# Three quarters of a weight load, issued behind the last residual stores instead of ahead of them, at the turn from one stage to the next

## The chip, the cores and the metric

The kernel runs on one core of a Trainium2 chip, as one launch. What counts is the device time of the execution, in microseconds (us). The core has five engines with a program each: TensorE (matmuls and transposes, called PE in the profile), VectorE (DVE), ScalarE (ACT), GpSimd (POOL) and SyncE (SP), which here only issues DMAs. ScalarE issues some DMAs too. All DMAs go through the core's 16 DMA engines. The engines wait for each other by semaphores.

## What is computed

The input x has 16 sequences of 1024 tokens, 512 features each, float32. A layer norm gives xn; the output is x plus a state-space block of xn plus a sparse expert block of xn:

```python
x = L0_attn_x
xn = _layernorm(x, axis=-1)
x = x + _L0_attn_ref(xn, W_in, dt_W, dt_b, A_log, D_param, W_out, norm_w) \
      + _L0_ffn_ref(xn, Wc, bc, W1, b1, W2, b2)
```

The second block takes the tokens in groups of 32. In each group each of 32 x 4 = 128 experts picks the token with its highest logit, by a one-hot matrix:

```python
logits = jnp.einsum('bntd,des->bntes', grouped, Wc) + bc
perm = (logits == jnp.max(logits, axis=-3, keepdims=True)).astype(x.dtype)
permuted = jnp.einsum('bntd,bntes->bnesd', grouped, perm)
inner = jax.nn.relu(jnp.einsum('bnesd,esdf->bnesf', permuted, W1) + b1)
result_permuted = jnp.einsum('bnesf,esdf->bnesd', inner, W2) + b2
result = jnp.einsum('bnesd,bntes->bntd', result_permuted, perm)
```

The first block ("attention" in the names of the code) is a projection, a scan over chunks of 64 tokens, a gate, a norm and an output projection.

## The kernel before

The kernel has three stages, one after the other in every engine's program: attention (to about 2070 us), gather (to about 2480 us) and scatter.

**Attention** walks over 64 super tiles of 256 tokens (NST = 64, two tiles of 128 each, 128 tiles in all), as a pipeline of three super tiles: at step s the projections of s, the scan of s - 1 and the output projection of s - 2. The last two steps, s = 64 and 65, only drain it. Per super tile it leaves in HBM: xn (normalised tokens, `xn_dram`), the one-hot matrix (`permT_dram`) and x plus the block's result, called the residual (`part_dram`). The residual of tile n is made by VectorE (`residual`, line 880) from output projection n into buffer `res[:, i]`, i = n mod 2, and SP stores it (`store_part`, line 368). The next residual into the same buffer waits until that store has landed (`res_out[i]`). Store (62,0) is that of tile 124, store (62,1) that of 125, (63,0) and (63,1) those of 126 and 127.

**Gather** works in 8 blocks (NGB) of 2048 tokens. A wave n = 4b + k is block b and the k-th of four slices of 128 features (KD = 4), so there are 32 waves. SP loads the tokens of a wave in four parts (tq) of four DMAs each, 64 KB apiece (`load_xn`, line 1292), into one of four buffers. TensorE's `pick` (n, tq) (line 1448, its matmuls at line 1462) multiplies a part by the one-hot matrix, 32 matmuls into one bank of PSUM; ScalarE (line 1389) and VectorE (`move_pick`, line 1391, copy at line 1393) each copy half of it to SBUF, and the next pick waits for both copies. Behind pick (n, tq) TensorE multiplies the picks of wave n - 1 by a slice of W1 (`apply_w1`, line 1469, matmuls at line 1486). W1, 8 MB, is loaded once, in four quarters by feature slice, 2 MB each (`load_w1`, line 1300). `apply_w1` of wave k waits for quarter k at its first use: quarter 0 behind pick (1,0), quarter 1 (the diff's k = 1) behind pick (2,0), and so on. The texts below count quarters 1 to 4 and waves 1 to 4 in words: quarter 2 of W1 is `load_w1(sync, 1)`, and the third wave is n = 2. In SBUF, W1 takes the place of attention's weights, so no quarter may be loaded before the last logits are projected (`lg_ps`).

**The turn.** The first picks are put between the last output projections: TensorE's order at the end is pick (0,0), transposes, projection 126, pick (0,1), projection 127, then pick (0,2), transposes of the second block's one-hot matrix (line 1445), pick (0,3), pick (1,0). VectorE's order is: copy of pick (0,0), residual 126, copy of pick (0,1), residual 127, copy of pick (0,2). The second block's transposes also wait for the last residual.

SP issues its DMAs in program order, and a wait in its program holds back all that is behind it. Its order at the turn, before the change: one-hot matrices of the first two blocks (8 DMAs), the first wave's tokens (16), quarter 1 of W1, the last store of the one-hot matrix, then `load_second`: the second wave's tokens (16) and quarters 2 to 4 of W1. Behind these come the four residual stores, each with its wait for the residual. The gather's own program (`sync_program`, line 1332) begins with waits for the last store of the one-hot matrix and for the last residual (`res_cp` at 2 * NST). Then come the tokens of the third and fourth waves, the permutation of the third block, and the loop that loads wave n + 4 as pick n goes on.

Of the kernel before, what the change touches and what calls it, by code (L numbers as in the profile page):

```python
# [31 lines left out]
KD = D // P  # L32
# [30 lines left out]
def wait(eng, sem, value):  # L63

    if not isinstance(value, int) or value > 0:
        eng.wait_ge(sem, value)
# [1154 lines left out]
def gather_phase(nc, io, keep, sems, att):  # L1221
# [67 lines left out]
    def quarter(i):  # L1289
        return slice(P // 4 * i, P // 4 * (i + 1))  # L1290

    def load_xn(sync, n, tq, i):
        tiles = slice(TW * tq, TW * tq + TW)
        sync.dma_start(xn[n % 4][quarter(i), tiles, :],
                       xn_dram[n // KD, n % KD][quarter(i), tiles, :]).then_inc(xn_in[n % 4][tq], 16)

    def load_perm(sync, b, i):
        sync.dma_start(permT[b % 2][quarter(i), :, :], perm_dram[b][quarter(i), :, :]).then_inc(perm_in[b % 2], 16)

    def load_w1(sync, k):  # L1300
        sync.dma_start(w1[:, k, :, :], io["w1"][:, k, :, :]).then_inc(w1_in[k], 16)
# [17 lines left out]
    def load_second(sync):  # L1319
        for tq in range(4):  # L1320
            for i in range(4):
                load_xn(sync, 1, tq, i)
        for k in range(1, KD):
            load_w1(sync, k)

    def store_inner(eng, b, piece):

        quads = slice(PQ * piece, PQ * piece + PQ)
        eng.wait_ge(biased, 2 * b + 1 + 2 * piece // PIECES)
        eng.dma_start(inner_dram[b][:, quads, :], inner[b % 2][:, quads, :]).then_inc(inner_out[b % 2], 16)  # L1330

    def sync_program(sync, scatter):
        for i in range(2):
            sync.wait_ge(att["pm_out"][i], 16 * (NST // 2))
        sync.wait_ge(att["res_cp"], 2 * NST)
        for n in range(2, 4):
            for tq in range(4):
                for i in range(4):
                    load_xn(sync, n, tq, i)
        sync.wait_ge(perm_ps, 1)  # L1340
        for i in range(4):
            load_perm(sync, 2, i)
        for e in range(4 * LAST):
            b, w = divmod(e, 4 * KD)
            sync.wait_ge(pick_ps, e + 1)
            for i in range(4):
                if i == 1:
                    wait(sync, w1_mid, e - 3)
                if i == 2:
                    sync.wait_ge(pick_cp[0], e + 1)  # L1350
                if i == 3 and e + 1 < 4 * LAST:
                    sync.wait_ge(pick_mid, e + 2)
                if e + 16 < 4 * LAST:
                    load_xn(sync, e // 4 + 4, e % 4, i)
            if b == NGB - 1 and w % 4 == 3:
                scatter["load_first"](sync, w // 4)
        for piece in range(PIECES // 2):
            store_inner(sync, NGB - 1, piece)
        for w in range(2):
            scatter["load_w2_next"](sync, w)  # L1360
        for piece in range(PIECES // 2, PIECES):
            store_inner(sync, NGB - 1, piece)
        for w in range(2, 4):
            scatter["load_w2_next"](sync, w)
# [103 lines left out]
    def tensor_program(pe, scatter):  # L1468
# [38 lines left out]
        for j in range(4):  # L1507
            scatter["apply_w2"](pe, j)
            apply_w1(LAST - 1, j)

    return dict(sync=sync_program, gpsimd=gpsimd_program, scalar=scalar_program, vector=vector_program, tensor=tensor_program,
                load_small=load_small, load_first=load_first, load_second=load_second, load_w1=load_w1, negate_b1=negate_b1,
                cast_ident=cast_ident, copy_perm=copy_perm, copy_pick=copy_pick, move_pick=move_pick, pick=pick,
                transpose_picks=transpose_picks,
# [370 lines left out]
```

## Time and profile before

| | |
|---|---|
| median of the runs | 3000.07 us |
| lowest and highest of the three | 2998.5, 3001.02 us |
| span of the profiled execution | 3002.6 us |
| TensorE busy (matmuls) | 2871.7 us, 96% |
| VectorE, ScalarE, GpSimd busy | 2053.3, 1713.5, 1430.4 us |
| DMA, mean over the span | 110 GB/s |

The profile is of one execution; all times are counted from the start of its span. Engines' busy times leave out register, semaphore and DMA-issuing instructions. TensorE's weight loads are an engine of their own in it (PEld). A row of a timeline gives the start, the duration, the engine, the line in the kernel, the operation with output and input, and how many instructions were merged; in brackets stands how long the engine was idle before and what ended that ("issue": nothing that the profile shows). SPq and ACTq are SP's and ScalarE's issues of DMAs; their duration is that of issuing, not of the transfer. Names with g_ belong to the gather and with s_ to the scatter; g_w is W1, g_xn a token buffer, g_picked the picks in SBUF.

### The profile page before, as it was taken

The numbers are of one execution on the slowest core, as the hardware profiler recorded it, in microseconds if no ns is written. First come the engines' busy times: TensorE is split into PE (matmuls) and PEld (weight loads), VectorE is DVE, ScalarE is ACT, GpSimd is POOL, SyncE is SP. The second block draws the span as 40 slices with busy tenths as digits, with TensorE's granted clock in tenths as the row PEclk, the third lists the DMA queues.
The fourth block names the chain that finished last, engine by engine and source line by source line (L and its number), as shares of the span: only waits on it lengthen the run. The fifth ranks groups of instructions, "written<-read, shape, count | busy, mean of one in ns | idle before, by whom it ended". The sixth has DMA issues, their size and how long they took to land.

```text
span 3002.6 us, 134681 instructions
## 1 busy us (share of the span) xinstructions
PE 2871.7 (96%) x59324; PEld 2453.1 (82%) x59324; DVE 2053.3 (68%) x2982; ACT 1713.5 (57%) x3751; POOL 1430.4 (48%) x2287
## 2 busy tenths in 40 slices
PE   8999999999999999999999999996787879999999
PEld 6888888888888888888888888885666668888887
DVE  5777777777777777777777777775444447777775
ACT  5665666666656666666566666663333335555555
POOL 4666676766666767667667666672010101101010
PEclk9999999999999999999999999998999999999999
DMA  4222222222222222222222222216444437877765
GB/s 150 77 74 71 77 78 75 76 74 77 74 71 79 76 76 76 70 80 74 72 79 74 80 71 71 81 46 214 131 134 119 115 110 217 235 218 223 225 206 156
DMA packets 372550, 328.99 MB, mean 110 GB/s; under 512 B 62960, under 2 KB 284656, under 8 KB 371328
## 3 DMA queue, kind: packets, MB, share of 16 engines
q1 hardware_dynamic: 362016, 310.21, 35.6%
q8 instruction: 469, 7.68, 1.1%
q10 hardware_dynamic: 9952, 10.17, 1.1%
q14 instruction: 113, 0.93, 0.1%
HBM read 206.96 MB, written 113.31 MB: 107 GB/s over the span
## 4 chain that ended last, share of the span: by engine, by line
PE 90%; DVE 4%; issue 3%; DMA 1%; SPq 1%; POOL 1%; ACT 0%; ACTq 0%; DVEq 0%; POOLq 0%
PE a_proj L992 40%; PE a_mix L992 11%; PE s_rt L1748 8%; PE g_pick_ps L1462 5%; PE a_scan L1106 5%; PE s_w_ps L1716 5%; PE s_rt L1761 4%; DVE g_picked L1393 3%; PE a_scan L1083 3%; PE a_scan L1070 2%; PE g_acc_ps L1486 2%; PE a_mix L1058 2%; PE a_misc L1050 1%; PE a_misc L1124 1%; DMA part_dram<-res 1%
## 5 line engine op out<-in xcount | busy, mean ns | idle before, releaser
L992 PE MATMUL a_proj<-wdh,xTh 128*128 128x512 f32 x1024 | 420.9, 411 | 5.0 <-issue 3.1
L1679 ACT COPY s_res<-s_rt 128x512 f32<-128x512 f32 x512 | 262.9, 601 | 245.8 <-PE s_rt L1748 245.8
L992 PE MATMUL a_proj<-wdh,xTl 128*128 128x512 f32 x1024 | 402.0, 393 | 0.0
L992 PE MATMUL a_proj<-wdl,xTh 128*128 128x512 f32 x1024 | 400.0, 391 | 1.5 <-issue 1.5
L824 DVE COPY_PREDICATED scan_in<-mask,a_scan 64x512 f32<-64x512 uint32 x512 | 382.3, 747 | 16.0
L1693 DVE TENSOR_TENSOR s_resT<-s_w_ps,s_b 128x1024 f32<-128x1024 f32 (+1 forms) x252 | 293.1, 1205 | 136.4 <-PE s_w_ps L1716 136.4
L465 POOL TENSOR_TENSOR dx<-xs,d_row 64x512 f32<-64x512 f32 x256 | 330.3, 1290 | 15.1
L640 ACT ACTIVATE scan_in<-CT,hsel 64x128 f32<-64x128 f32 x1024 | 326.0, 388 | 4.9
L473 POOL TENSOR_TENSOR yv<-yt,dx 128x512 f32<-128x512 f32 x128 | 188.6, 1473 | 292.8 <-DVE yt L864 292.8
L604 ACT ACTIVATE raw<-a_proj,rs 128x272 f32<-128x272 f32 x128 | 62.5, 488 | 427.6 <-PE a_proj L992 427.6
L1393 DVE COPY g_picked<-g_pick_ps 128x1024 f32<-128x1024 f32 x128 | 156.7, 1224 | 216.3 <-PE g_pick_ps L1462 216.3
L884 DVE SCALAR_TENSOR_TENSOR res<-a_mix,rms,x 128x512 f32<-128x512 f32 x127 | 95.4, 751 | 270.9 <-PE a_mix L992 258.6
L456 POOL TENSOR_TENSOR scan_in<-CT,hsel 64x512 f32<-64x512 f32 x256 | 269.0, 1051 | 10.0
L1389 ACT COPY g_picked<-g_pick_ps 128x1024 f32<-128x1024 f32 x128 | 129.6, 1012 | 248.4 <-PE g_pick_ps L1462 247.8
L1748 PE MATMUL s_rt<-s_ident,s_resT 128*128 128x128 f32 x2048 | 254.7, 278 | 0.9 <-DVE s_resT L1693 0.5
L616 ACT ACTIVATE xs<-a_proj,rs 64x512 f32<-64x512 f32 x256 | 174.8, 683 | 125.0 <-PE a_proj L992 123.4
L1748 PEld LDWEIGHTS s_rt<-s_ident,s_resT 128*128 128x128 f32 x2048 | 219.0, 140 | 31.6 <-issue 25.1
L992 PEld LDWEIGHTS a_proj<-wdh,xTh 128*128 128x128 f32 x1024 | 192.2, 188 | 47.5 <-issue 10.8
L992 PEld LDWEIGHTS a_proj<-wdh,xTl 128*128 128x128 f32 x1024 | 192.3, 188 | 45.4 <-issue 1.9
L992 PE MATMUL a_proj<-xTh,wth 128*128 128x256 f32 x768 | 222.1, 289 | 0.0
L992 PEld LDWEIGHTS a_proj<-wdl,xTh 128*128 128x128 f32 x1024 | 193.0, 188 | 35.2 <-issue 2.9
L992 PE MATMUL a_proj<-xTh,wtl 128*128 128x256 f32 x768 | 216.3, 282 | 0.0
(153 smaller groups left out, 7104.4 us busy)
## 6 DMA issues: line engine op xcount, KB each, us to landing
x<-in_x_dram SPq DMA_DIRECT2D x128, 256.0 KB, 2.7
xn_dram<-xn SPq DMA_DIRECT2D x128, 256.0 KB, 2.4
part_dram<-res SPq DMA_DIRECT2D x128, 256.0 KB, 2.5
g_xn<-xn_dram SPq DMA_DIRECT2D x512, 64.0 KB, 2.3
s_w<-in_w_dram SPq DMA_DIRECT2D x128, 256.0 KB, 4.1
s_part<-part_dram SPq DMA_DIRECT2D x128, 256.0 KB, 3.9
out_dram<-s_out SPq DMA_DIRECT2D x128, 256.0 KB, 3.0
xr<-in_xT_dram SPq DMA_DIRECT2D x126, 256.0 KB, 2.8
```

Of the source, the lines that this page charges most:

```text
L456: nc.gpsimd.tensor_tensor(c_places(1, w), src, sel, ALU.mult).then_inc(cs_cp[1], 1)
L465: nc.gpsimd.tensor_tensor(dx[rows_, :], xs[c][n % 4][rows_, :, :].rearrange("t h d -> t (h d)"), d_row[rows_, :], ALU.mult).then_inc(dx_cp, 1)
L473: nc.gpsimd.tensor_tensor(yv[:], yt[:], dx[:], ALU.add).then_inc(yv_cp, 1)
L616: last = nc.scalar.activation(xs[c][n % 4][rows_, :, :], proj[0][rows_, :].rearrange("p (h d) -> p h d", h=H), ACT.Copy, scale=inv(n, rows_))
L640: last = nc.scalar.activation(dst[:, :, j, :], CT[own, n % 4, :, 0:CH], ACT.Copy, scale=hsel4[own, j:j + 1])
L824: nc.vector.copy_predicated(dst, mask[rows_, :].unsqueeze(1).unsqueeze(1).to_broadcast([CH, 4, 2, CH]), src).then_inc(mt_cp, 1)
L992: last = nc.tensor.matmul(out, lhs[a], rhs[c], start=(k == 0 and n == 0), stop=(k == nk - 1 and n == 2))
L1106: last = nc.tensor.matmul(out, scan_in[c][:, h, i:i + 32], xs[c][n % 4][:, h, :], start=True, stop=True)
L1393: nc.vector.tensor_copy(picked_view(n, tq, 1), pick_view(1)).then_inc(pick_cp[1], 1)
L1679: nc.scalar.copy(res[:, n % 4, :, :], rt_bank[:, n % 3, :, :]).then_inc(res_cp, 1)
L1693: last = nc.vector.tensor_tensor(resT[m % 2][j][:, :, sets].rearrange("p n (q r) -> p n q r", r=4)[:, :, :, 0:r], w2_place(u)[:, 0:r, :, j ...
L1748: last = nc.tensor.transpose(rt_bank[:, n % 3, g, :], resT[m % 2][j][:, place, :], ident[:])
```

## The change

`load_second` no longer issues quarters 2 to 4 of W1. The gather's program on SP issues them behind its waits for the last residual, the first of them ahead of the third wave's tokens, the second between the third and the fourth wave's, the third behind these. The set of DMAs is the same. No other engine's program changes.

```diff
@@ -1320,8 +1320,6 @@
         for tq in range(4):
             for i in range(4):
                 load_xn(sync, 1, tq, i)
-        for k in range(1, KD):
-            load_w1(sync, k)
@@ -1333,10 +1331,12 @@
         for i in range(2):
             sync.wait_ge(att["pm_out"][i], 16 * (NST // 2))
         sync.wait_ge(att["res_cp"], 2 * NST)
-        for n in range(2, 4):
-            for tq in range(4):
-                for i in range(4):
-                    load_xn(sync, n, tq, i)
+        for k in range(1, KD):
+            load_w1(sync, k)
+            if k < KD - 1:
+                for tq in range(4):
+                    for i in range(4):
+                        load_xn(sync, k + 1, tq, i)
         sync.wait_ge(perm_ps, 1)
```

## Rows read from the trace of the kernel before

**Rows 1.** The page, busy tenths of TensorE in 40 equal slices of the span.
```profile
PE   8999999999999999999999999996787879999999
```

**Rows 2.** Chain that ended last, 2040 to 2080 us: start, us, what.
```profile
2057.89 19.27 DMA part_dram<-res
```

**Rows 3.** Timeline of SP's issues, 2020 to 2120 us.
```profile
2047.43 0.43 SPq L1301 DMA_DIRECT2D g_w<-in_w_dram  x1
...
2056.47 1.37 SPq L1301 DMA_DIRECT2D g_w<-in_w_dram  x3
2057.89 22.67 SPq L370 DMA_DIRECT2D part_dram<-res  x4
2080.67 18.01 SPq L1294 DMA_DIRECT2D g_xn<-xn_dram  x32
```

**Rows 4.** DMA issues 2050 to 2060 us: count, KB each, median us to landing.
```profile
g_w<-in_w_dram SPq DMA_DIRECT2D x3, 2048.0 KB, 14.7
```

**Rows 5.** Timeline of VectorE at the turn.
```profile
2077.63 0.75 DVE L884 SCALAR_TENSOR_TENSOR res<-a_mix,rms,x 128x512 f32<-128x512 f32 x1 [12.31 <-DMA part_dram<-res]
2078.30 1.21 DVE L1393 COPY g_picked<-g_pick_ps 128x1024 f32<-128x1024 f32 x1
```

**Rows 6.** Timeline of TensorE at the turn.
```profile
2039.86 1.05 PE L1445 MATMUL g_acc_ps<-g_ident,g_permT 128*128 128x128 bf16 x16 [0.97 <-DMA g_permT<-permT_dram]
...
2070.13 0.40 PE L992 MATMUL a_misc<-woh,yll 128*128 128x512 f32 x1
2079.66 2.09 PE L1462 MATMUL g_pick_ps<-g_perm,g_xn 32*128 32x128 f32 x32 [9.13 <-DVE g_picked L1393]
...
2087.03 1.17 PE L1462 MATMUL g_pick_ps<-g_perm,g_xn 32*128 32x128 f32 x32 [1.44 <-DVE g_picked L1393]
```

**Rows 7.** Stretch of 2 us: PE busy, granted clock, DMA share, GB/s.
```profile
2076.00:2078.00 2.00, 0.00 (x0) 0.50 0.10 31
```

**Rows 8.** DMA issues in 2047.77 to 2048.71 us: KB each, us to landing.
```profile
g_w<-in_w_dram SPq DMA_DIRECT2D x1, 2048.0 KB, 10.4
...
g_xn<-xn_dram SPq DMA_DIRECT2D x1, 64.0 KB, 6.9
```

**Rows 9.** Timeline of TensorE in the gather's first waves.
```profile
2094.80 0.75 PE L1486 MATMUL g_acc_ps<-g_picked,g_w 128*32 128x64 f32 x36 [0.39 <-issue]
...
2096.59 1.08 PE L1486 MATMUL g_acc_ps<-g_picked,g_w 128*32 128x64 f32 x59
2099.13 0.31 PE L1486 MATMUL g_acc_ps<-g_picked,g_w 128*32 128x64 f32 x5 [1.46 <-issue]
2099.37 1.18 PE L1462 MATMUL g_pick_ps<-g_perm,g_xn 32*128 32x128 f32 x32
```

**Rows 10.** DMA by queue, 2100 to 2200 us: packets, MB, share of 16 engines.
```profile
q8 instruction: 25, 0.41, 1.9%
```

**Rows 11.** Waits of TensorE, 2100 to 2200 us: us in total, times, longest.
```profile
PE g_acc_ps L1486 <- issue: 9.6, 11, 2.1
...
PE g_pick_ps L1462 <- issue: 2.6, 4, 1.3
```

**Rows 12.** DMA 2060 to 2070 us, packets of all queues.
```profile
DMA packets 293, 4.16 MB, mean 416 GB/s; under 512 B 34, under 2 KB 34, under 8 KB 40
```

**Rows 13.** Timeline of TensorE as the scatter's first loads go out.
```profile
2435.08 0.95 PE L1462 MATMUL g_pick_ps<-g_perm,g_xn 32*128 32x128 f32 x23 [1.06 <-issue]
...
2439.42 0.99 PE L1486 MATMUL g_acc_ps<-g_picked,g_w 128*32 128x64 f32 x55 [0.50 <-issue]
...
2444.47 0.87 PE L1486 MATMUL g_acc_ps<-g_picked,g_w 128*32 128x64 f32 x24 [2.27 <-issue]
```

**Rows 14.** Stretch of 4 us: PE busy, granted clock, DMA share, GB/s.
```profile
2440.00:2444.00 4.00, 2.20 (x101) 1.00 0.99 340
```

**Rows 15.** DMA by queue, 2440.5 to 2444.5 us.
```profile
q1 hardware_dynamic: 646, 1.19, 81.9%
```

**Rows 16.** The page, DMA issues: count, KB each, median us to landing.
```profile
g_xn<-xn_dram SPq DMA_DIRECT2D x512, 64.0 KB, 2.3
```

## The prediction

> **What bounds the kernel now.** First the page's slices of 75 us: TensorE is busy nine tenths or more in attention and scatter and seven or eight tenths in the gather between; the lowest (6) is the slice from 2027 to 2102 us, the turn from attention to gather [rows 1]. The chain that ended last goes into the transfer of a residual store there and stays in it for 19.27 us [rows 2]. SP's timeline tells what lies before that store: the issues of W1's quarters 2 to 4, at 2056.47, with the first of four residual stores at 2057.89 [rows 3]. The three quarters land in a median of 14.7 us [rows 4], the store only after them: it stands in line behind 6 MB. VectorE's residual of tile 126 needs that store's buffer and sits idle 12.31 us for it, until 2077.63; behind it on VectorE is the copy of the picks (line 1393), and TensorE's pick (0,2) sits idle 9.13 us for that copy [rows 5, 6]. [...]
>
> **What the change takes away.** Without three W1 issues ahead of it, store (62,0) is issued at about 2056.5 instead of 2057.9. Only the first W1 quarter (issued 2047.43, 10.4 us, thus landed at 2057.8) and the second wave's tokens lie before it. It must land by 2066.3, when projection 126 is done; with the 6.9 us of a token load behind a quarter [rows 8] it lands at 2063.4. The other store before the end, (62,1), is issued at about 2059.1 and needed at 2070.5. No wait is left there.
> The new chain, each step from a row:
> - projection 127 ends at 2070.5 as before (last matmul 2070.13, 0.40) [rows 6]. Pick (0,2) follows at once, since its bank's copy is made while projection 127 runs: 2070.4 to 2071.5. I take full clock, as TensorE comes from four busy microseconds and more, with no gap before it.
> - residual 127 (0.75 us) to 2071.35; transposes of the second block 1.05 us as those at 2039.86, to 2072.5. VectorE's copy of pick (0,2) 1.22 us [rows 5, 6] after the residual, 2071.65 to 2072.9. Pick (0,3) 2073.1 to 2074.3, its copy to 2075.6, pick (1,0) at 2075.8.
> Before, pick (1,0) starts at 2087.03 [rows 6]. **The gain up to there is 11.2 us**: 9.3 of waiting (2079.66 against 2070.4) and 1.9 for work and clock. From pick (1,0) on the order of TensorE's work is the same in both.
>
> **What the change adds: the data.** No wait is new, but W1's quarters 2 to 4 now stand behind SP's wait for all residuals (about 2071.4), and the tokens of waves 3 and 4 stand between them.
> - SP issues a token load in 0.56 us (32 in 18.01) and a quarter in 0.45 (1.37 for three) [rows 3]. So quarter 2 goes out at 2071.9, 16 loads of wave 3 until 2081.4, quarter 3 there, 16 loads of wave 4 until 2090.9, quarter 4 there, four of the permutation until 2093.1, and then the loop for the fifth wave and on.
> - A quarter with a wave of tokens behind it landed in 10.4 us [rows 8]; those issued in a row in 14.7, the median [rows 4]. Quarter 2 lands at 2082.3 to 2086.6 and is first read behind pick (2,0), which is four picks after 2075.8. Before, these four took 12.34 us (2087.03 to 2099.37) [rows 6, 9], so quarter 2 is needed at 2089.3 at the earliest: 3 to 7 us to spare. Quarter 3 lands at 2091.8 to 2096.1, needed behind pick (3,0) at 2101 or later; quarter 4 at 2101.3 to 2105.6, needed behind pick (4,0), 2112 or later. Tokens of wave 3, part one: issued by 2074.6, landed at 6.9 us, 2081.5, needed at 2088. The loop's first load (wave 5) is issued at 2093.1 and needed at about 2111. Covered, all of them; if one isn't, TensorE, and behind it both copies, stand still for the remainder.
> - ScalarE issues four permutation loads of its own from pick (1,0) on. They aren't waited for before the ninth wave.
>
> **What the change adds: company for the code.** This is the term that I price against the gain. TensorE gets its instructions by DMA as well: the queue named instruction carried 25 packets with 0.41 MB from 2100 to 2200 us, 16.4 KB each [rows 10]. In the gather stage TensorE halts in the middle of a group, for "issue": at 2094.80, and again at 2099.13, with 36 matmuls, a pick of 32 and 59 more between, 127 in all [rows 9]. 127 matmuls with their weight loads are 254 instructions, a block of code. From 2100 to 2200 us these halts sum to 9.6 + 2.6 = 12.2 us [rows 11], 0.49 for each of the 25 packets. So in the gather the next block arrives just about when it is needed, and whatever slows its transfer is paid in full. (In the scatter TensorE is nine tenths busy or more [rows 1], so there it does not matter.)
> Before, W1 passed while TensorE ran the last projections or stood still, few instructions a microsecond. In the changed kernel it passes beside the densest code. From 2071.9 to about 2101 the DMA engines have 6 MB, which at 4.16 MB in 10 us [rows 12] is 15 us out of 29, and between them 32 and more token loads in small packets: about full.
> The nearest rows for a gather stage with full DMA are those where the scatter's first loads go out: 2434 to 2444, at the end with a share of 0.99. Its three halts are 1.06, 0.50 and 2.27 us, 1.28 each [rows 13, 14]. How many blocks begin in the loaded stretch? Pick (1,0) at 2075.8 to 2101, a block each 4.2 us: six. Six at 1.28 are 7.7 us; six at the 0.49 of before are 2.9. **The loss with traffic like that one is 4.8 us**; the low end is 0, if it was only the mix of queues there that did the harm. For the high end: packets of W1 are large, 4.16 MB in 293 [rows 12], 14 KB, where those of 2440 were 1.8 KB (1.19 MB in 646) [rows 15]. Sixteen engines for 10 us over 293 packets are 0.54 us a packet. One such packet ahead of each block adds 6 x 0.54 = 3.2, so 8.0 us; two make 11.3, the high end. I take the middle of 4.8 and 8.0, **6.4 us**, as the load of 2440 is the nearest and one packet ahead of a block the plainest addition. A clock that falls after a long halt, as at 2079.66 (0.9 us on one pick), costs 1 us more and is only in the range.
> Sum: -11.2 + 6.4 = -4.8 us. The profiled execution spans 3002.6 us, 0.08% above the median of 3000.07; I take the difference from the median: **2995.3 us**.
>
> [...] The halts [rows 9, 11] are there without W1 already. [...]
> [...] No row shows a code block behind a W1 packet.
>
> **Rivals.**
> 1. The code comes in time all the same. For it: the waits count 15 halts for 25 blocks [rows 10, 11], so ten blocks came in time. Against: the three halts at full share [rows 13]. Loss 0 to 3 us, time 2988.9 to 2991.9. Chance 0.22.
> 2. Code behind W1 (the slower side). If a block waits as a token load does behind a quarter, 6.9 us [rows 8] instead of 2.3 [rows 16], it comes 4.6 us later. [...] Place: blocks from 2076 to 2101 us. The point from which it decides: the kernel loses when six blocks lose over 11.2 us together, 1.9 each, and is slower by over 0.2% from 2.9 each. At 3.5 each, 21 us: 3010. Against it: the token loads stand in W1's own queue, code in another. Chance 0.10; a middle course (loss of 9 to 17 us, 2998 to 3006) 0.09.
> 3. A quarter or a wave lands late, as DMA is full and SP issues in order: at 5 us over the 14.7 [rows 4], quarter 2 would land at 2091.6, 2 us late, and the others likewise: 2997 to 3002. Against: no other quarter is ahead of it. Chance 0.05.
> 4. The change doesn't take: store (62,0) is still late behind quarter 1 and the tokens, as these share the engines until 2060 or so; then residual 126 waits as before. It would have to land 10 us later than the token loads beside it. 3000. Chance 0.04.
> The forecast (loss of 3 to 9 us, 2991.9 to 2998) has the remaining 0.50.
>
> **How the numbers follow.** What a measurement of this kernel can tell from no change is about 0.2%, 6 us: faster means below 2994.1, slower above 3006.1. Faster: rival 1 (0.22) and four tenths of the forecast (0.20), 0.42. Slower: rival 2 and a rest of the middle, 0.12. Same: 0.46. The range leaves out rival 2 and the top of the middle course: 2988.5 to 3003.
>
> **What the trace after would show.** The first step is right if VectorE's residual 126 starts at about 2066.4 without a wait for the residual store, and pick (0,2) at 2070.4, at full clock. The second, if pick (1,0) starts at about 2075.8. The third, if SP's issues of W1 lie at about 2072, 2081 and 2091 and TensorE waits for neither W1 nor tokens. The fourth, the price, if the halts for "issue" in the first 25 us from pick (1,0) sum to 8 to 11 us where six blocks of before have 2.9; at under 5 it is rival 1, at over 20 rival 2. From pick (5,0) on both kernels should run in parallel, with a constant offset of 5 us. The prediction is wrong if that offset changes later, or if a wait at the turn stays that I put down to the store.

## The result and the profile after

The changed kernel takes 3007.53 us (median of 20 runs), the kernel before, on the same chips, 3001.91 (20 runs): a ratio of 1.0017, 95% interval 1.0010 to 1.0023. That is 5.1 us slower on 3000: small, inside the 0.2% that was called no change, but clear of 1 by the interval, and in the other direction than forecast. 3000.07 x 1.0017 is 3005.2, which is 2.2 us above the end of the range (3003) and 9.9 above the forecast of 2995.3. The profiled execution spans 3005.8 us, against 3002.6 before.

The stores no longer stand in line. SP's issues at the turn (start, us, line, what, count):

```profile
2058.60 15.20 SPq L370 DMA_DIRECT2D part_dram<-res  x4
2073.92 0.43 SPq L1301 DMA_DIRECT2D g_w<-in_w_dram  x1
...
2082.71 0.43 SPq L1301 DMA_DIRECT2D g_w<-in_w_dram  x1
...
2091.24 0.43 SPq L1301 DMA_DIRECT2D g_w<-in_w_dram  x1
...
2093.57 36.24 SPq L1294 DMA_DIRECT2D g_xn<-xn_dram  x63
```

VectorE in the changed kernel: residuals 126 and 127 (line 884), which now wait for projections alone, and the copies of picks (0,2), (1,0) and (4,0).

```profile
2068.57 0.75 DVE L884 SCALAR_TENSOR_TENSOR res<-a_mix,rms,x 128x512 f32<-128x512 f32 x1 [1.14 <-PE a_mix L992]
2072.67 0.75 DVE L884 SCALAR_TENSOR_TENSOR res<-a_misc,rms,x 128x512 f32<-128x512 f32 x1 [1.74 <-PE a_misc L992]
2073.87 1.22 DVE L1393 COPY g_picked<-g_pick_ps 128x1024 f32<-128x1024 f32 x1 [0.45 <-PE g_pick_ps L1462]
...
2079.07 1.23 DVE L1393 COPY g_picked<-g_pick_ps 128x1024 f32<-128x1024 f32 x1 [1.38 <-PE g_pick_ps L1462]
...
2130.74 1.23 DVE L1393 COPY g_picked<-g_pick_ps 128x1024 f32<-128x1024 f32 x1 [2.44 <-PE g_pick_ps L1462]
```

The wait of 12.31 us [rows 5] is gone. The turn came 2.1 us later in this execution, which has nothing to do with the change: in attention, near 1000 us, the execution is already 1.8 us behind. So I count from VectorE's first copy of a pick, (0,0): it starts at 2063.10 before and at 2065.21 after. From there, the copy of pick (1,0) starts after 25.16 us before (2088.26) and after 13.86 now (2079.07): 11.3 us gained. But from the copy of (1,0) to that of (4,0), which I call **the stretch**, it was 35.49 us (2088.26 to 2123.75) and is 51.67 now (2079.07 to 2130.74): 16.2 us lost. From TensorE's timeline in the stretch:

```profile
2080.44 1.16 PE L1462 MATMUL g_pick_ps<-g_perm,g_xn 32*128 32x128 f32 x28 [0.40 <-DVE g_picked L1393]
2083.85 0.49 PE L1462 MATMUL g_pick_ps<-g_perm,g_xn 32*128 32x128 f32 x4 [2.25 <-issue]
...
2087.76 1.07 PE L1486 MATMUL g_acc_ps<-g_picked,g_w 128*32 128x64 f32 x28
2090.62 0.75 PE L1486 MATMUL g_acc_ps<-g_picked,g_w 128*32 128x64 f32 x36 [1.79 <-issue]
...
2092.41 1.08 PE L1486 MATMUL g_acc_ps<-g_picked,g_w 128*32 128x64 f32 x59
2098.20 0.43 PE L1486 MATMUL g_acc_ps<-g_picked,g_w 128*32 128x64 f32 x5 [4.71 <-issue]
2098.57 2.09 PE L1462 MATMUL g_pick_ps<-g_perm,g_xn 32*128 32x128 f32 x32
...
2105.09 0.50 PE L1462 MATMUL g_pick_ps<-g_perm,g_xn 32*128 32x128 f32 x6 [1.38 <-issue]
...
2112.70 1.13 PE L1486 MATMUL g_acc_ps<-g_picked,g_w 128*32 128x64 f32 x39 [4.00 <-issue]
2113.76 2.09 PE L1462 MATMUL g_pick_ps<-g_perm,g_xn 32*128 32x128 f32 x32
```

These lines answer to [rows 9]. The halts are in the middle of a group, and in the code TensorE's waits stand only ahead of one, so a wait for data isn't their cause. The longest is 4.71 us where 1.46 was; the five sum to 14.13 us. After three of them (2.25, 4.71 and 4.00 us) the next pick takes 2.09 us instead of 1.17, at a granted clock of 0.50; after the first, 68 matmuls at full clock lie between. Three stretches of 2 us, with TensorE's busy time, granted clock, DMA share and GB/s among the columns:

```profile
2082.00:2084.00 2.00, 0.15 (x3) 0.15 (x3) 0.00 (x0) 0.00 (x0) 0.00 (x0) 1.00 1.06 259
...
2096.00:2098.00 2.00, 0.00 (x0) 0.00 (x0) 0.00 (x0) 0.00 (x0) 0.00 (x0) 0.50 0.91 283
...
2110.00:2112.00 2.00, 0.00 (x0) 0.00 (x0) 0.00 (x0) 0.00 (x0) 0.00 (x0) 1.00 1.09 286
```

All engines but the DMA engines stand still. DMA issues from 2080 to 2085 us in the changed kernel (KB each, us to landing) show how long a transfer then takes, in SP's queue and in ScalarE's:

```profile
g_w<-in_w_dram SPq DMA_DIRECT2D x1, 2048.0 KB, 11.1
g_xn<-xn_dram SPq DMA_DIRECT2D x9, 64.0 KB, 6.3
g_permT<-permT_dram ACTq DMA_DIRECT2D x1, 128.0 KB, 8.2
```

The last line is the one I should have asked for: a load in another queue than W1's takes 8.2 us, where the median of such loads was 2.9 before, in the list of all DMA issues of the kernel:

```profile
g_permT<-permT_dram ACTq DMA_DIRECT2D x20, 128.0 KB, 2.9
```

The copy of pick (5,0) starts 73.08 us after the first copy before and 78.24 now, 5.2 us later. That this equals the 5.1 us of the ratio is luck, for the offset of these two executions doesn't stay: at the copy of pick (7,3) it is 2.8 us (112.02 against 109.22), at (15,3) 0.3 and at the last, (31,3), 1.4 (403.66 against 402.22). The spans differ by 3.2 us, 2.1 of them from before the turn. Single executions wander by 2 us and more in the rest of the gather; that the kernel lost about 5 us rests on the 20 runs of each, not on the two traces.

### The profile page after: what moved, and what is told of

It is laid out like the page before. It is cut to its first block, busy times and chain, and to the rows that moved or that the text cites. A ratio compares the mean times of both kernels' runs of the same rounds, so it can differ in the third digit from the quotient of the medians.

```text
span 3005.8 us, 134681 instructions
## 1 busy us (share of the span) xinstructions
PE 2871.7 (96%) x59324; PEld 2452.7 (82%) x59324; DVE 2052.4 (68%) x2982; ACT 1714.4 (57%) x3751; POOL 1432.8 (48%) x2287
## 3 DMA queue, kind: packets, MB, share of 16 engines
q8 instruction: 469, 7.68, 1.1%
## 4 chain that ended last, share of the span: by engine, by line
PE 90%; DVE 5%; issue 4%; POOL 1%; ACT 0%; DMA 0%; ACTq 0%; SPq 0%; POOLq 0%; DVEq 0%
PE a_proj L992 40%; PE a_mix L992 11%; PE s_rt L1748 8%; PE g_pick_ps L1462 5%; PE a_scan L1106 5%; PE s_w_ps L1716 5%; PE s_rt L1761 4%; DVE g_picked L1393 3%; PE a_scan L1083 3%; PE a_scan L1070 2%; PE g_acc_ps L1486 2%; PE a_mix L1058 2%; PE a_misc L1050 1%; PE a_misc L1124 1%; PE a_misc L1114 0%
## 5 line engine op out<-in xcount | busy, mean ns | idle before, releaser
L824 DVE COPY_PREDICATED scan_in<-mask,a_scan 64x512 f32<-64x512 uint32 x512 | 382.1, 746 | 16.1
L1376 POOL TENSOR_TENSOR g_inner<-g_inner,g_b 128x1024 f32<-128x1024 f32 x16 | 30.5, 1903 | 391.0 <-DVE g_inner L1420 391.0
```

Of the source, the lines that this page charges most:

```text
L824: nc.vector.copy_predicated(dst, mask[rows_, :].unsqueeze(1).unsqueeze(1).to_broadcast([CH, 4, 2, CH]), src).then_inc(mt_cp, 1)
```

## The experiments

All are compared with the kernel before by the ratio of the times. The stretch is read in each trace from the starts of the two copies, so it is that of one execution each. How far it can be trusted shows in the row of the shifted code: the changed kernel's work and traffic, and a stretch that is 4.1 us shorter. Where two stretches differ by less than about 4 us, the traces alone don't tell the kernels apart; the intervals of the ratios decide.

| kernel | stretch, us | copy (0,0) to (4,0), us | ratio to before | 95% interval |
|---|---|---|---|---|
| before | 35.5 | 60.7 | 1 | |
| changed | 51.7 | 65.5 | 1.0017 | 1.0010 to 1.0023 |
| changed, code shifted (one run) | 47.6 | 61.5 | not timed | |
| one quarter of W1 in all | 35.3 | 50.6 | 0.9966 | 0.9954 to 0.9979 |
| rows of 2 KB | 44.1 | 57.9 | 1.0000 | 0.9991 to 1.0009 |
| between the stores | 38.1 | 52.9 | 0.9975 | 0.9966 to 0.9984 |
| in a row | 47.8 | 63.2 | 1.0001 | 0.9992 to 1.0010 |
| one quarter late | 41.0 | 54.9 | 0.9979 | 0.9969 to 0.9988 |
| spread, rows of 2 KB | 42.6 | 56.4 | 0.9990 | 0.9977 to 1.0002 |
| between the stores, rows of 2 KB | 37.2 | 52.5 | 0.9972 | 0.9960 to 0.9983 |

### Without quarters 2 to 4 of W1

```diff
     def load_w1(sync, k):
-        sync.dma_start(w1[:, k, :, :], io["w1"][:, k, :, :]).then_inc(w1_in[k], 16)
+        sync.dma_start(w1[:, 3, :, :], io["w1"][:, 3, :, :]).then_inc(w1_in[k], 16)
...
         for k in range(1, KD):
-            load_w1(sync, k)
             if k < KD - 1:
...
-            if b == 0 and j == 0:
-                pe.wait_ge(w1_in[k], 16)
+            if n == 0 and j == 0:
+                pe.wait_ge(w1_in[0], 16)
...
-  acc_bank[ES * e:ES * e + ES, j, c, :], w1[:, k, 4 * q + e, :],
+  acc_bank[ES * e:ES * e + ES, j, c, :], w1[:, 3, 4 * q + e, :],
```

> Quarters 2 to 4 of W1 are not loaded at all, and every apply_w1 reads the one quarter that is (so the expert block's numbers are not the reference's); the rest is the changed kernel. Theory C (W1's traffic delays TensorE's code): from the last scan of attention to pick (4,0), 64.3 us in the trace of before and 69.1 in that of after, it takes 64.3 - 11.3 = 53 us; halts for issue in the first 25 us of picks under 5 us in sum; the kernel is 11 us faster than before (2990.6) and 16 faster than the changed one. Rival D (the loss has another source, such as tokens of waves 3 and 4 issued nearer to the picks, or W1 data arriving late, which would be gone too, but not the token part): the halts stay over 8 us and the gain over before is under 6 us.

The stretch is 35.3 us, as before the change, though picks and tokens stand as near to each other as in the changed kernel. Waits of TensorE from 2058 to 2125 us:

```profile
PE g_acc_ps L1485 <- issue: 4.3, 5, 1.4
...
PE g_pick_ps L1461 <- issue: 0.9, 2, 0.6
```

The time is 0.34% under that of before, 10.2 us (5 runs; the interval allows 6 to 14), and 0.51% under the changed kernel, if the two ratios are divided: 15 us. So the loss comes with the transfer of quarters 2 to 4, and the turn itself is worth 10.2 us by the time, for 11.2 forecast. Rival D is out. (The expectation counts from the last scan, the table from the first copy.)

### Which code: the same kernel with its code shifted

The longest halts stand 127 or so matmuls apart. To see whether they belong to the code or to events at those picks, the code was pushed back.

```diff
         pe.wait_ge(zeroed, 5)
-        warm_up(6)
+        warm_up(36)
```

> The changed kernel, with 30 more of the matmuls that warm TensorE up at the very start. [...] Theory C (a halt is the wait for the next block of code): in the changed kernel TensorE halts after 28 of 32 matmuls of pick (1,1), after 28 of 64 of the W1 matmuls two picks on, and after 59 of 64 one more on; here the same halts stand 30 matmuls earlier, that is after 62 of 64 W1 matmuls behind pick (1,0), then 127 on, at about 30 of 32 of pick (1,3) (30 before place 28 of 64), and 127 on, after 29 of 64. Their lengths are like those of before, 1 to 5 us. Rival F (the halts belong to events of data, semaphores or ports, not to code): they stay at the same matmuls, 28 of 32 in pick (1,1) and so on. The time as a whole grows by up to 6 us for the warm-up.

TensorE's timeline of the shifted kernel:

```profile
2083.73 1.10 PE L1486 MATMUL g_acc_ps<-g_picked,g_w 128*32 128x64 f32 x64
2088.19 2.09 PE L1462 MATMUL g_pick_ps<-g_perm,g_xn 32*128 32x128 f32 x32 [3.36 <-issue]
...
2091.72 1.17 PE L1462 MATMUL g_pick_ps<-g_perm,g_xn 32*128 32x128 f32 x31
2094.66 0.27 PE L1462 MATMUL g_pick_ps<-g_perm,g_xn 32*128 32x128 f32 x1 [1.78 <-issue]
...
2099.80 0.72 PE L1486 MATMUL g_acc_ps<-g_picked,g_w 128*32 128x64 f32 x34 [1.72 <-issue]
...
2107.22 0.42 PE L1486 MATMUL g_acc_ps<-g_picked,g_w 128*32 128x64 f32 x2 [4.58 <-issue]
```

Of the changed kernel's halts, the one after 28 of 64 W1 matmuls behind pick (1,2) now stands ahead of that pick; the one after 59 of 64 behind pick (1,3) stands after 31 of 32 within it; that after 26 of 32 of pick (2,1) stands after 30 of 64 of the group ahead of it; that after 25 of 64 behind pick (2,2) stands after 62 of 64 of the group ahead of that pick. Each has moved by 59 or 60 matmuls. My number of 30 was wrong by a factor of two: each warm-up matmul of the program stands in the profile as two (12 records for 6 at the kernel's start, and 59384 matmuls in all instead of 59324 for 30 more), and the distance shows that they are two matmuls in the code as well: 30 more calls are 60 more matmuls. The halts move with the code; rival F is out. What they wait for shows in the queue named instruction. In all it carries 469 packets with 7.68 MB in the changed kernel, for 59324 matmuls and as many weight loads, 253 a packet; in the shifted one, with 60 more of each, it is 470. From 2080 to 2113 us the changed kernel has five:

```profile
q8 instruction: 5, 0.08, 1.1%
```

They start at 2081.1, 2087.9, 2095.6, 2102.3 and 2110.1 us (to 0.1 us), one to each of the five long halts and 2.6 to 2.8 us ahead of its end. In the shifted kernel four start from 2080 to 2108 us, 2.5 to 2.9 us ahead of the ends of its halts at 2088.19, 2094.66, 2099.80 and 2107.22. So I read a long halt as the wait for a block of TensorE's code of 16.4 KB; in the two longest of the changed kernel the block's transfer starts 2.1 and 1.4 us after TensorE has stopped (at 2093.49 and 2108.70).

The changed kernel's first halt (after 28 of 32 of pick (1,1), 2.25 us) has no counterpart: at its new place, 60 matmuls earlier, no halt is seen. The halts that remain are as long as before (up to 4.58 us), but there is a long one less, all over 0.2 us up to pick (4,0) sum to 13.7 us instead of 16.1, and the stretch is 47.6 us instead of 51.7. So where the borders fall, or chance between executions, is worth 4 us of the stretch. This is one execution, with no timed comparison.

### The size of W1's rows

```diff
     def load_w1(sync, k):
-        sync.dma_start(w1[:, k, :, :], io["w1"][:, k, :, :]).then_inc(w1_in[k], 16)
+        step = EX if k == 0 else 16
+        for e in range(0, EX, step):
+            sync.dma_start(w1[:, k, e:e + step, :], io["w1"][:, k, e:e + step, :]).then_inc(w1_in[k], 16)
...
-                pe.wait_ge(w1_in[k], 16)
+                pe.wait_ge(w1_in[k], 16 if k == 0 else 128)
```

> The changed kernel, each of quarters 2 to 4 issued as eight DMAs of 2 KB a partition in a row instead of one with 16 KB a partition. Bytes and place are the same, packets are an eighth as large. Theory P (the size of W1's packets is what a code block waits for): the halts from pick (1,0) to (4,0) fall from 14.6 us to about 8 (1.28 for each of six blocks as in the gather's end), and the time to pick (4,0) from 69.1 to about 62; 5 to 7 us faster than the changed kernel, even with before or a little faster. Rival Q (the amount in the queues counts, not the packet): halts stay at 12 to 16 us, time as the changed kernel within 2 us. SP needs 21 more issues of 0.45 us, 9 us, which has room.

From 2076 to 2080 us, packets of all queues, first the changed kernel, then this one:

```profile
DMA packets 96, 1.57 MB, mean 393 GB/s; under 512 B 0, under 2 KB 0, under 8 KB 0
```
```profile
DMA packets 740, 1.35 MB, mean 338 GB/s; under 512 B 80, under 2 KB 80, under 8 KB 740
```

The stretch falls from 51.7 to 44.1 us and the time by 0.17% (1.0017 to 1.0000, intervals that don't overlap). The halts over 0.2 us up to pick (4,0) sum to 7.9 us instead of 16.1. Loads in ScalarE's queue issued from 2074 to 2094 us, where the changed kernel's three took a median of 8.2 us, take 4.5:

```profile
g_permT<-permT_dram ACTq DMA_DIRECT2D x3, 128.0 KB, 4.5
```

In the shifted kernel, again with rows of 16 KB, the three such loads issued from 2076 to 2096 us took 6.5, so part of the distance between 8.2 and 4.5 may be chance. Theory P, which had the halts at about 8 us and the kernel 5 to 7 us faster, holds: by the stretch 7.6 of the 16.4 us that W1 adds come with large rows, by the time 5 of 15. The rest comes with small ones too, so P isn't all.

The edit changes a second thing, which stands against reading all of this as the size of the rows. SP needs 3.8 to 4.7 us for the eight issues of a quarter, so quarters 3 and 4 go out at 2087.4 and 2101.1 us instead of 2082.7 and 2091.2, and from 2074 to 2094 us the DMA engines move 259 GB/s at a share of 0.83, where the changed kernel has 318 at full share. The next experiment has small rows at a share of 0.94 (255 GB/s) in these 20 us, and its stretch is no longer; that speaks for the rows.

### Spread among the tokens

```diff
+        def piece(j):
+            k, e = 1 + j // 8, j % 8 * 16
+            sync.dma_start(w1[:, k, e:e + 16, :], io["w1"][:, k, e:e + 16, :]).then_inc(w1_in[k], 16)
+        loads = [(n, tq, i) for n in range(2, 4) for tq in range(4) for i in range(4)]
+        for j in range(24):
+            piece(j)
+            for load in loads[4 * j // 3:4 * (j + 1) // 3]:
+                load_xn(sync, *load)
```

> The changed kernel, with quarters 2 to 4 cut into eight DMAs each (2 KB a partition) that are spread among the 32 token loads of waves 3 and 4, three DMAs of W1 for four of tokens, so that no burst of W1 is longer than 256 KB. Bytes in the stretch are those of the changed kernel. With 2 KB rows in bursts of 2 MB the stretch from the copy of pick (1,0) to (4,0) was 44.1 us, with 16 KB rows 51.7. Theory B (a code block waits for the burst that is in the queues): halts of under 1.3 us each, the stretch 39 to 42 us, 2 to 4 us faster than the kernel with 2 KB rows. Rival Q2 (with small rows it is the share of the DMA engines alone): 43 to 46 us as there.

42.6 us is between the two expectations, and the ratio, 0.9990, has an interval (0.9977 to 1.0002) that overlaps with that of the bursts (0.9991 to 1.0009). The longest halt is still 2.79 us, which B had at under 1.3:

```profile
2091.38 0.43 PE L1488 MATMUL g_acc_ps<-g_picked,g_w 128*32 128x64 f32 x5 [2.79 <-issue]
```

The halts over 0.2 us sum to 9.1 us, not less than the 7.9 of the bursts. So theory B isn't borne out, and a gain from spreading isn't shown: 1.5 us of the stretch is less than two executions can differ by. What is left would then be the amount beside the code, which was not varied by itself at this size of rows.

### The order among the late quarters and the tokens

```diff
         for k in range(1, KD):
             load_w1(sync, k)
-            if k < KD - 1:
-                for tq in range(4):
-                    for i in range(4):
-                        load_xn(sync, k + 1, tq, i)
+        for n in range(2, 4):
+            for tq in range(4):
+                for i in range(4):
+                    load_xn(sync, n, tq, i)
```

> The changed kernel, with the three quarters in a row ahead of the tokens of waves 3 and 4, so only the order among these is undone. Theory C: the same bytes meet the same code, but in one burst of 15 us from 2072 on, in which three or four blocks are late instead of six, and the tokens of wave 3 stand behind 6 MB: they land at 2090 or later, where pick (2,0) comes at about 2089 to 2094. Time to pick (4,0) 66 to 72 us, same as the changed kernel within 3 us. If a wait for tokens of wave 3 of over 3 us appears, the tokens between are what this order is worth. Rival P: as here only W1's own packets are ahead of code, halts per block should be longest of all (over 4 us).

The stretch is 47.8 us, 3.9 less than in the changed kernel, and the time 0.16% less, by intervals that just touch (0.9992 to 1.0010 and 1.0010 to 1.0023). The wait for tokens exists, but is short:

```profile
2087.74 1.28 PE L1486 MATMUL g_acc_ps<-g_picked,g_w 128*32 128x64 f32 x36 [2.59 <-issue]
2095.72 0.43 PE L1486 MATMUL g_acc_ps<-g_picked,g_w 128*32 128x64 f32 x5 [3.77 <-issue]
2097.72 2.09 PE L1462 MATMUL g_pick_ps<-g_perm,g_xn 32*128 32x128 f32 x32 [1.57 <-DMA g_xn<-xn_dram]
```

The halts are no longer than in the changed kernel, and fewer are long. Rival P in its plain form, with halts of over 4 us when only W1's packets are ahead of the code, isn't seen. The tokens between the quarters, which the change took care to put there, save nothing by the time and probably cost some us. A reading that fits, but wasn't tested: they make W1's passage longer, so that more blocks of code meet it.

### A dose of one

Quarters 2 and 3 early (as in the next experiment), quarter 4 late. The diff is against the changed kernel.

```diff
             if valid(s - 2):
                 store_part(s - 2, 1)
+            if s == NST:
+                for k in range(1, 3):
+                    gather["load_w1"](sync, k)
...
-        for k in range(1, KD):
-            load_w1(sync, k)
-            if k < KD - 1:
-                for tq in range(4):
-                    for i in range(4):
-                        load_xn(sync, k + 1, tq, i)
+        for n in range(2, 4):
+            for tq in range(4):
+                for i in range(4):
+                    load_xn(sync, n, tq, i)
+        load_w1(sync, 3)
```

> A dose: quarters 2 and 3 of W1 go between residual stores (62,1) and (63,0), quarter 4 alone goes out late, behind the tokens of waves 3 and 4 (at about 2093 us). Theory C, that each late quarter costs by its own traffic beside the picks: from the copy of pick (1,0) to that of (4,0), 35.3 us with no late quarter and 51.7 with three, it takes about 36 plus one third of 16.4, 41 to 42 us; against the kernel with all three between the stores (38.1) 2 to 5 us more, with one halt of over 2 us within 10 us of the issue of quarter 4, and none from 2080 to 2092. Time 2 to 4 us over that kernel, still 3 to 5 below before. Rival E (the loss comes once, from the pile of the first late quarter, and further ones are nearly free): 45 us or more.

The stretch is 41.0 us, as computed; the ratio is 0.9979. The quarter is issued at 2090.77 in this trace. Behind that come two halts of over 2 us, where one was expected, the second 13.7 us after the issue; ahead of it the longest is 1.40 us:

```profile
2087.43 0.31 PE L1488 MATMUL g_acc_ps<-g_picked,g_w 128*32 128x64 f32 x5 [1.40 <-issue]
...
2097.75 1.06 PE L1488 MATMUL g_acc_ps<-g_picked,g_w 128*32 128x64 f32 x39 [2.91 <-issue]
...
2104.51 0.32 PE L1488 MATMUL g_acc_ps<-g_picked,g_w 128*32 128x64 f32 x7 [2.41 <-issue]
```

By the stretch, one late quarter costs 2.9 us over the kernel with all three early; the time, expected 2 to 4 us longer, differs by 0.04%, which is too small to tell. Rival E is out: the kernel is 0.38% faster than the changed one, so the loss didn't come with the first late quarter.

### A version that keeps the gain

The last two residual stores are waited for by nobody before the scatter. So W1 can go between (62,1) and (63,0): behind the stores that matter, and ahead of the dense code. The diff is against the changed kernel.

```diff
             if valid(s - 2):
                 store_part(s - 2, 1)
+            if s == NST:
+                for k in range(1, 4):
+                    gather["load_w1"](sync, k)
...
-        for k in range(1, KD):
-            load_w1(sync, k)
-            if k < KD - 1:
-                for tq in range(4):
-                    for i in range(4):
-                        load_xn(sync, k + 1, tq, i)
+        for n in range(2, 4):
+            for tq in range(4):
+                for i in range(4):
+                    load_xn(sync, n, tq, i)
```

> Quarters 2 to 4 of W1 are issued in a row behind residual store (62,1) and ahead of (63,0): the two stores that somebody waits for are ahead of W1, the two that nobody waits for before the scatter behind it, and W1 passes from about 2061 on, beside the last projections. Theory C: no residual waits, as in the changed kernel; W1 is through by 2076 to 2078 (15 to 17 us), so only the first one or two code blocks of the picks meet it, at 2 to 4 us in sum. Time from the last scan to pick (4,0) 54 to 58 us, 6 to 10 us faster than before, 2992 to 2996. Rival D: the loss comes with the picks' nearness to the tokens: 62 us or more, no faster than before.

SP's issues in it, and TensorE from pick (1,0) on:

```profile
2058.24 3.07 SPq L370 DMA_DIRECT2D part_dram<-res  x2
2061.36 2.54 SPq L1304 DMA_DIRECT2D g_w<-in_w_dram  x3
2069.10 4.45 SPq L370 DMA_DIRECT2D part_dram<-res  x2
```
```profile
2077.57 2.09 PE L1463 MATMUL g_pick_ps<-g_perm,g_xn 32*128 32x128 f32 x32 [1.43 <-DVE g_picked L1394]
...
2084.26 0.78 PE L1463 MATMUL g_pick_ps<-g_perm,g_xn 32*128 32x128 f32 x4 [1.88 <-issue]
```

VectorE's residuals wait for no store here either. In the trace one halt of 1.88 us and a stretch of slow work are left: pick (1,0) takes 2.09 us, with no halt ahead of it but the 1.43 us of waiting for a copy that stand there in the changed kernel too, and after the halt the clock is low once more (0.58 from 2084 to 2086 us; the group of 64 behind the pick takes 1.94 us instead of 1.10). How much of the half clock is W1's doing isn't shown. The ratio to before is 0.9975 (0.9966 to 0.9984), 7.5 us faster, and 12.6 us faster than the changed kernel. With rows of 2 KB as well:

> The kernel with the three quarters between the residual stores, each quarter as eight DMAs with 2 KB a partition. If the size of W1's rows is what the first code blocks of the picks wait for, the slow pick at 2077.6 (clock) and the halt of 1.88 us at 2084.3 go, and the stretch from the copy of pick (1,0) to (4,0) falls from 38.1 to 36 us: 1 to 2 us faster. Against it: the 24 issues take 11 us of SP, which end at about 2073, so residual stores and tokens of wave 3 go out 3 to 4 us later and W1 passes over a longer stretch: then even with the other, or 1 us slower.

The stretch is 37.2 us instead of 38.1, the ratio 0.9972 (0.9960 to 0.9983): not to be told from the other by time or stretch. Pick (1,0) is at full clock now (1.17 us), as expected, but the halt stays and a slow pick follows it:

```profile
2075.12 1.17 PE L1465 MATMUL g_pick_ps<-g_perm,g_xn 32*128 32x128 f32 x32 [1.43 <-DVE g_picked L1396]
...
2080.51 0.49 PE L1465 MATMUL g_pick_ps<-g_perm,g_xn 32*128 32x128 f32 x4 [1.62 <-issue]
...
2082.75 1.96 PE L1465 MATMUL g_pick_ps<-g_perm,g_xn 32*128 32x128 f32 x32
```

Either version beats both kernels.

## Why the prediction was wrong

- **The wait and its removal: right.** Counted from the first copy, residual 126 starts 11.2 us sooner (3.36 instead of 14.53 us behind it) and the copy of pick (1,0) 11.3 us sooner, for 11.2 predicted (10.2 by the time, in the kernel without quarters 2 to 4). TensorE's steps from (0,2) to (1,0) took full clock, as assumed: 1.17 us for each of the three picks, with a granted clock of 1.00 from 2070 to 2076 us, where it was 0.50 in the idle time before the change [rows 7].
- **The data are covered: right.** TensorE waits for no quarter and no tokens in the changed kernel. SP's issues at 2073.9, 2082.7 and 2091.2, less the 2.1 us of the later turn, lie at 2071.8, 2080.6 and 2089.1, for 2071.9, 2081.4 and 2090.9 predicted.
- **That TensorE's code is what pays: right in kind.** The long halts go with the transfer of W1's quarters, they move with the code, and each ends 2.5 to 2.9 us after a packet of the queue named instruction has started. The shifted kernel too shows halts of up to 4.58 us at the borders of its blocks. Rival 1 fell.
- **The price: wrong, and it is the term that failed.** The sum had +6.4 us for W1's company. It measured 15 us by the time (changed kernel against the one without quarters 2 to 4) and 16.4 by the stretch; -11.3 and +16.2 against before give the +5 that was measured. I had six blocks at 1.28 to 1.82 us, 9.3 in the middle, less 2.9 of before, and left the clock out. Four things were mis-sized. (1) The *single halt*: the five long ones sum to 14.13 us, a mean of 2.83, about twice what I had. (2) The *number of blocks*: up to 2103 us here, my 2101, only three long halts fall and not six, as long halts slow the pace at which the code runs. They sum to 8.75 us (2.25, 1.79, 4.71), inside the 8 to 11 that I had named as the sign of being right, but that is luck: two errors cancel. (3) The *length of the loaded stretch*: the DMA engines stay full until 2112 (a share of 1.09 from 2110 on, 0.71 in the 2 us behind), as SP, behind with its tokens, issues 63 loads in 36 us without a pause; another 1.38 and 4.00 us of halts fall there. (4) The *clock*: it falls after three of the halts. All halts over 0.2 us up to pick (4,0) sum to 16.07 in the changed kernel and to 4.02 without W1's quarters, so 12.05 of the 16.4 us are halts; the rest, 4.3 us, I put down to work at half clock (three picks at 2.09 instead of 1.17 are 2.8 of it, and a group of W1 matmuls at 1.94 instead of 1.10 is 0.8). That share is read off one trace, not tested.
- **The sign that I named for later: it turned.** I wrote that the prediction is wrong if the offset changes after pick (5,0). It was +5.2 us there, not -5, and it fell to 0.3 by pick (15,3). In other pairs of traces it moves by 2 us or so as well, so two single executions couldn't have served as that sign.
- **The argument that held rival 2 down: wrong.** I wrote that the token loads stand in W1's own queue and code in another. The loads in ScalarE's queue, also another, took 8.2 us instead of 2.9. Rival 2's own price, 4.6 us a block, was reached by one halt (4.71); its sum of 21 us went by 3.5 a block, for which I gave no row. The size of W1's packets accounts for a third of the loss by the time and under half by the stretch, as far as the small rows test it alone. The size is that of what I called the middle course (loss of 9 to 17 us), to which I gave 0.09. The term of one W1 packet of 0.54 us ahead of each block was never seen as such: no view shows a code block behind a W1 packet, and one packet a block was my estimate. What the runs show in its place are the halts: five with W1 beside the code, of 2.83 us in the mean, and 4.02 us of halts in all without quarters 2 to 4.
- The rest of the loss, which stays with small rows, is measured (10 us by the time, 8.8 by the stretch) but not explained: blocks come late then too, at a DMA share of 0.83 to 0.94. Whether a code transfer waits at the DMA engines or at the memory, no run here tells.

## What to carry to other kernels

A bulk load that is moved out of the way of a store is still to be paid for where it lands. Look for a place beside long instructions, as here the last projections, and keep it away from the stretch where an engine runs through its code fastest and already halts at even distances (here 127 matmuls). Ask of each store in the queue who waits for it; here two of the four had nobody, and the load belonged ahead of those. To price traffic beside code, look at a small load in another queue beside it (here 8.2 us instead of 2.9), not at the queue's names, and cost the clock together with the halts.

## What the runs showed of the hardware

- TensorE's halts follow its code. Pushed back by 60 matmuls, they moved by 59 or 60, and they grew with DMA traffic: 4.0 us in the stretch without W1's quarters, 16.1 with them (13.7 with the code shifted).
- The queue named instruction goes with TensorE's code: 469 packets of 16.4 KB for 118648 matmuls and weight loads, 253 a packet. The five long halts of the changed kernel, 127 or 128 matmuls apart, each end 2.6 to 2.8 us after such a packet has started.
- Loads of 128 KB in ScalarE's queue took 8.2 us beside rows of 16 KB in SP's queue (6.5 in the shifted kernel), 4.5 beside rows of 2 KB and 2.9 over the whole kernel before. Each of the first three is the median of three loads; from 2074 to 2094 us the changed kernel moved 318 GB/s and that with small rows 259.
- During a halt of 4.71 us the granted clock went from 1.00 to 0.50, and the next pick ran at 2.09 us instead of 1.17.
